# A fused attention and wave layer on one Trainium2 core: first loads, first rotation and slot transfers reordered and joined

## The reference, cut to what matters

```python
x = x + attn(layernorm(x))          # x: 4 x 2048 x 256 f32
x = x + ffn(layernorm(x))
# attn: qkv = x @ w_qkv; 16 heads of 16 dims; rotary embedding on Q and K;
#       softmax(Q K^T / 4, causal) V, then @ w_proj + b_proj
# ffn:  sqrt((x @ cos(theta + theta_noise))^2 + (x @ sin(phi + phi_noise))^2)
```

## Time and profile before

| | |
|---|---|
| median of 3 runs | 2236.44 us (2230.28 to 2236.95) |
| the profiled execution, its own time | 2240.03 us |
| its span, first to last instruction | 2238.3 us |
| mean granted TensorE clock | 0.966 of full speed |
| PE busy | 2070.9 us (93%) |
| VectorE (DVE) busy | 1601.9 us (72%) |
| ScalarE (ACT) busy | 1296.1 us (58%) |
| POOL (GpSimd) busy | 870.6 us (39%) |
| DMA moved | 159.87 MB, 71 GB/s on the mean |

### The profile page before, as it was taken

The page is one execution under the profiler, slowest core; times in us unless marked ns, Lnnn a source line. Parts: engine busy times, 40 slices in busy tenths (PEclk is TensorE's granted clock), DMA queues, the critical chain, the costliest instruction groups (busy, mean ns, idle before and its releaser), DMA issues.

```text
span 2238.3 us, 37555 instructions
## 1 busy us (share of the span) xinstructions
PE 2070.9 (93%) x12864; PEld 869.9 (39%) x12864; DVE 1601.9 (72%) x2868; ACT 1296.1 (58%) x1620; POOL 870.6 (39%) x1250
## 2 busy tenths in 40 slices
PE   4999999989999999999999999999999999999883
PEld 3333333334433344334443344334444344333331
DVE  4787777877778778787677767687777777778611
ACT  1346656655566565666567555665656565566571
POOL 4622324352444325343534434335244434432331
PEclk9889999999999999999999999999999999999996
DMA  5420222132212223222222222122122211221211
GB/s 159 115 62 23 73 61 88 42 103 60 82 55 80 61 61 88 65 84 87 75 70 77 72 65 79 58 75 84 56 77 71 81 60 52 73 72 32 78 58 43
DMA packets 119561, 159.87 MB, mean 71 GB/s; under 512 B 30662, under 2 KB 82246, under 8 KB 119110
## 3 DMA queue, kind: packets, MB, share of 16 engines
q1 hardware_dynamic: 118928, 155.22, 23.7%
q10 hardware_dynamic: 444, 2.26, 0.3%
HBM read 88.97 MB, written 50.86 MB: 62 GB/s over the span
## 4 chain that ended last, share of the span: by engine, by line
PE 62%; DMA 7%; DVE 7%; issue 7%; POOL 7%; ACT 5%; SPq 4%; POOLq 0%; DVEq 0%
PE banks L761 16%; PE banks L745 15%; PE banks L724 15%; PE banks L685 5%; DVE chunk_max L943 4%; PE banks L694 3%; ACT probs L831 3%; DMA rot<-raw 3%; PE banks L675 2%; PE banks L722 2%; DMA inverse<-inverses 2%; SPq L508 2%; PE banks L708 2%; POOL crossed L478 1%; SPq L525 1%
## 5 line engine op out<-in xcount | busy, mean ns | idle before, releaser
L943 DVE TENSOR_REDUCE chunk_max<-banks 128x1 f32<-128x512 f32 (+3 forms) x2240 | 1399.8, 671 | 433.6 <-PE banks L724 418.9
L831 ACT ACTIVATE probs<-banks 128x1024 f32<-128x1024 f32 (+3 forms) x1280 | 1074.7, 899 | 567.5 <-PE banks L745 543.1
L724 PE MATMUL banks<-stack_k,stack_q 96*128 96x512 bf16 (+3 forms) x2560 | 833.7, 357 | 35.3 <-DVE chunk_max L943 27.6
L745 PE MATMUL banks<-stack_q,stack_k 99*128 99x512 bf16 (+3 forms) x2560 | 694.4, 353 | 15.9 <-ACT probs L831 7.0
L761 PE MATMUL banks<-probs,v_one 128*17 128x512 f32 (+3 forms) x5120 | 539.0, 537 | 21.4 <-POOL probs L1078 20.2
L724 PEld LDWEIGHTS banks<-stack_k,stack_q 96*128 96x128 bf16 x2560 | 249.3, 99 | 406.2 <-DVE chunk_max L943 183.5
L745 PEld LDWEIGHTS banks<-stack_q,stack_k 99*128 99x128 bf16 x2560 | 220.9, 99 | 280.7 <-ACT probs L831 127.5
L1078 POOL TENSOR_SCALAR_AFFINE_SELECT probs<-probs 128x512 f32<-128x512 f32 x256 | 166.3, 655 | 314.1 <-ACT probs L831 307.8
L761 PEld LDWEIGHTS banks<-probs,v_one 128*17 128x17 f32 x5120 | 117.7, 97 | 303.0 <-issue 224.2
L722 PE MATMUL banks<-diag_mask,ident_bf 128*128 128x128 bf16 x1024 | 204.9, 225 | 12.7 <-DVE chunk_max L943 9.1
L722 PEld LDWEIGHTS banks<-diag_mask,ident_bf 128*128 128x128 bf16 x1024 | 100.3, 99 | 148.2 <-DVE chunk_max L943 75.3
(11 more groups left out here) (88 smaller groups left out, 1134.3 us busy)
## 6 DMA issues: line engine op xcount, KB each, us to landing
split<-parts SPq DMA_DIRECT2D x64, 384.0 KB, 2.6
stack_q<-split SPq DMA_DIRECT2D x384, 64.0 KB, 2.2
stack_k<-split SPq DMA_DIRECT2D x384, 64.0 KB, 2.2
rot<-raw SPq DMA_DIRECT2D x256, 64.0 KB, 2.0
sums<-o_raw SPq DMA_DIRECT2D x64, 256.0 KB, 2.1
xin<-x SPq DMA_DIRECT2D x16, 512.0 KB, 4.0
heads_t<-sums SPq DMA_DIRECT2D x28, 256.0 KB
mid<-x SPq DMA_DIRECT2D x14, 512.0 KB, 4.1
```

What stands on the lines that cost most here:

```text
L724: mm = nc.tensor.matmul(bank[:, n * wide:(n + 1) * wide], stack_q[u % 2][0:SPLIT_ROWS, t, h + n, j * P:(j + 1) * P], stack_k[u % 2][0:SPLI ...
L745: mm = nc.tensor.matmul(scores_bank[h][:, w0:SPAN], stack_k[u % 2][0:ROWS, j // SUB, h, (j % SUB) * P:(j % SUB + 1) * P], stack_q[u % 2][0 ...
L831: nc.scalar.activation(probs[:, g % PROBS, 2 * pair:2 * pair + 2, w0:SPAN], scores_pair[pair][:, :, w0:SPAN], ACT.Exp).then_inc(s_exp, 1)
L943: nc.vector.tensor_reduce(to, bank[:, 0:count * wide].rearrange("p (h n) -> p h n", h=count), AX.X, ALU.max).then_inc(s_emptied["DVE"], 1)
```

## The change

It does nine things. The statistics of block 1 wait for the normalisation of block 0. The query and key weights are loaded as the first group and the other three, the tables as the first span's columns and the rest; PE and the rotation wait for each at its first use. In the first rotation two of the four half swaps are issued on ScalarE's queue, and its seven VectorE operations are planned with no lag between them. fetch_slots issues six copies where it issued twelve: a run of slots with the same part is one copy with a broadcast source, a run with successive parts one copy with the parts as its first dimension. The value products of a unit wait in the plan for its query and key product, and unit 1's first products for unit 0's rows. The planner's costs of SP's jobs are raised. SLACK goes from 0.2 to 0.4. A change of type on PE is put off within 3 us of the last one (STICK, RUN). The split's result is planned as usable 1.0 us later (TURN_LAG). The change is described as having the value products two steps at a time; VALUES is 2 on both sides of the diff.

```diff
+SLOT_RUNS = ((0, 0, 0, 3, True), (0, 3, 1, 2, True), (0, 5, 2, 1, True), (1, 0, 0, 3, False), (1, 3, 0, 2, False), (1, 5, 0, 1, True))
+HALVES = ((0, 32), (32, 0), (64, 96), (96, 64))
-LOADS = 2 * SLOTS * 16
+LOADS = len(SLOT_RUNS) * 16
-SLACK = 0.2
+SLACK = 0.4
+STICK = 0.05
+RUN = 3.0
+TURN_LAG = 1.0
...
-            job(("xload", n), "SP", 0.1, at, [("xt", n - 2, 1)], 4.2)
-            job(("stats", n), "DVE", 2.1, at, [("xload", n), ("apply", n - 2), begun(at - SLACK)])
+            job(("xload", n), "SP", 0.45, at, [("xt", n - 2, 1)], (4.8, 8.0)[n] if n < 2 else 4.2)
+            job(("stats", n), "DVE", 2.1, at, [("xload", n), ("apply", n - 2), *([("apply", 0)] if n == 1 else []), begun(at - SLACK)])
...
-            job(("rot", u, c), "SP", 0.3, at, [("out", ("qk", u, c, 1)), ("rope", *ago, 1)], 2.4)
+            job(("rot", u, c), "SP", 2.4 if i else 1.2, at, [("out", ("qk", u, c, 1)), ("rope", *ago, 1)], 1.8)
...
-                    job(("rope", u, c, n), "DVE", 0.68, at, after)
+                    job(("rope", u, c, n), "DVE", 0.8, at, after, 0.0 if n < ROPE_OPS - 1 else None)
...
-            job(("keep", u, c), "SP", 0.1, at, [("rope", u, c, ROPE_OPS - 1), ("fetch", *ago)], 2.4)
-            job(("fetch", u, c), "SP", 1.0, at, [("keep", u, c), ("scores", u - 2, NSTEP - 1, 1)], 4.0)
+            job(("keep", u, c), "SP", 0.45, at, [("rope", u, c, ROPE_OPS - 1), ("fetch", *ago)], 2.4)
+            job(("fetch", u, c), "SP", 2.7, at, [("keep", u, c), ("scores", u - 2, NSTEP - 1, 1)], 2.2)
...
-            job(("split", u, c), "POOL", 1.3, at - 0.2, [("rowmax", u, c)])
+            job(("split", u, c), "POOL", 1.3, at - 0.2, [("rowmax", u, c)], TURN_LAG if u else None)
...
-            job(("rows", u, c), "SP", 0.3, at, [("out", ("turn", u, c))], 2.4)
+            job(("rows", u, c), "SP", 1.7, at, [("out", ("turn", u, c))], 1.8)
...
-            found.append((max(at, free[e]) + TURN_COST * change, jobs[name][2], name))
+            stick = STICK * change if free[e] - since < RUN else 0.0
+            found.append((max(at, free[e]) + TURN_COST * change, jobs[name][2] + stick, name))
...
-                    for at in range(0, P, P // 2):
-                        for own, other in ((at, at + 32), (at + 32, at)):
-                            sp.dma_start(rot[own:own + 32, i % 2, :], raw[other:other + 32, i % 2, :]).then_inc(s_rot[i % 2], 16)
+                    for own, other in HALVES[0:2] if i == 0 else HALVES:
+                        sp.dma_start(rot[own:own + 32, i % 2, :], raw[other:other + 32, i % 2, :]).then_inc(s_rot[i % 2], 16)
...
-                    for side, (tile, which) in enumerate(((stack_q, Q_PARTS), (stack_k, K_PARTS))):
-                        for slot, part in enumerate(which):
-                            rows = split[i % 2, part, side * P // 2:(side + 1) * P // 2, :]
-                            sp.dma_start(tile[u % 2][slot * HD:(slot + 1) * HD, c, :, :],
-                                         rows.rearrange("(d h) n -> d h n", h=HG)).then_inc(s_fetch[i % 2], 16)
+                    for side, slot, part, count, same in SLOT_RUNS:
+                        rows = split[i % 2, part:part + (1 if same else count), side * P // 2:(side + 1) * P // 2, :]
+                        if same:
+                            rows = rows.to_broadcast([count, P // 2, SPAN])
+                        tile = (stack_q, stack_k)[side][u % 2][slot * HD:(slot + count) * HD, c, :, :]
+                        sp.dma_start(tile.rearrange("p h n -> p (h n)"), rows.rearrange("m (d h) n -> m d (h n)", h=HG)).then_inc(s_fetch[i % 2], 16)
...
-                sp.dma_start(wqk[:, :, :, :], w_qk.rearrange("g p k n -> p g k n")).then_inc(s_wqk, 16)
+                sp.dma_start(wqk[:, 0, :, :], w_qk[0]).then_inc(s_wqk[0], 16)
                 load_block(1)
                 sp.dma_start(wv[:, :, :], w_v.rearrange("(k p) n -> p k n", p=P)).then_inc(s_wv, 16)
+                sp.dma_start(wqk[:, 1:GROUPS, :, :], w_qk[1:GROUPS].rearrange("g p k n -> p g k n")).then_inc(s_wqk[1], 16)
...
+                        if i == 0:
+                            ins.then_inc(s_emptied["ACT"], 1)
+                            emptied(act, item)
+                            for own, other in HALVES[2:4]:
+                                act.dma_start(rot[own:own + 32, 0, :], raw[other:other + 32, 0, :]).then_inc(s_rot[0], 16)
+                            return
...
-                act.dma_start(cos_t[:, :], cosines).then_inc(s_tables, 16)
-                act.dma_start(sin_t[:, :], sines).then_inc(s_tables, 16)
+                for n, columns in enumerate((slice(0, SPAN), slice(SPAN, SEQ))):
+                    act.dma_start(cos_t[:, columns], cosines[:, columns]).then_inc(s_tables[n], 16)
+                    act.dma_start(sin_t[:, columns], sines[:, columns]).then_inc(s_tables[n], 16)
```

More of the change, by code:

```diff
@@ L166, in plan @@
             for k in range(KT):
-                job(("qk", u, c, k), "PE", 0.86, at - HOLD * k, [("out", ("xt", n, k)), before_qk, ("rope", *ago, 1), begun(at - SLACK)])
+                job(("qk", u, c, k), "PE", 0.86, at - HOLD * k, [("out", ("xt", n, k)), before_qk, ("rope", *ago, 1), begun(at - SLACK), ("rows", u - 1, c) if u == 1 else begun(at - SLACK)])
                 before_qk = ("qk", u, c, k)
             with_bank(("qk", u, c, 0), ("qk", u, c, 1), "ACT", 0.5, at, [("rope", *ago, 1)])
-            job(("rot", u, c), "SP", 0.3, at, [("out", ("qk", u, c, 1)), ("rope", *ago, 1)], 2.4)
+            job(("rot", u, c), "SP", 2.4 if i else 1.2, at, [("out", ("qk", u, c, 1)), ("rope", *ago, 1)], 1.8)
             last = ((i - 1) // SPANS, (i - 1) % SPANS)
@@ L212, in plan @@
             free = [("qk", UNITS - 1, SPANS - 1, KT - 1), ("v", PAIRS - 1, SPANS - 1, SUB - 1)] if finish_set(n) else []
-            job(("den", n), "SP", 0.1, at, [("store", unit, t), ("keepinv", prev), ("den", n - 1), begun(at - SLACK)], 2.2)
-            job(("heads", n), "SP", 0.2, at, [("store", unit, t), ("wave", prev, SUB - 1), ("sin", KT - 1), ("heads", n - 1), *free], 2.5)
-            job(("x3", n), "SP", 0.1, at, [("final", prev), ("x3", n - 1), begun(at - SLACK), *free], 4.2)
+            job(("den", n), "SP", 0.5, at, [("store", unit, t), ("keepinv", prev), ("den", n - 1), begun(at - SLACK)], 2.2)
+            job(("heads", n), "SP", 1.1, at, [("store", unit, t), ("wave", prev, SUB - 1), ("sin", KT - 1), ("heads", n - 1), *free], 2.5)
+            job(("x3", n), "SP", 0.45, at, [("final", prev), ("x3", n - 1), begun(at - SLACK), *free], 4.2)
             job(("bias", n), "POOL", 1.3, at, [("x3", n), ("bias", n - 1)])
             job(("invert", n), "DVE", 0.5, at, [("den", n), ("invert", n - 1)])
-            job(("keepinv", n), "SP", 0.1, at, [("invert", n), ("keepinv", n - 1)], 2.2)
-            job(("inverse", n), "SP", 0.2, at, [("keepinv", n), ("add", prev), ("inverse", n - 1), *free], 2.5)
+            job(("keepinv", n), "SP", 0.35, at, [("invert", n), ("keepinv", n - 1)], 2.2)
+            job(("inverse", n), "SP", 1.1, at, [("keepinv", n), ("add", prev), ("inverse", n - 1), *free], 4.5)
             job(("scale", n), "DVE", 1.25, at, [("heads", n), ("inverse", n), ("scale", n - 1)])
@@ L262, in plan @@
             job(("lift", u, t), "ACT", 0.6, at - 0.1, [before_values])
-            job(("store", u, t), "SP", 0.1, at, [("lift", u, t)], 2.4)
+            job(("store", u, t), "SP", 0.35, at, [("lift", u, t)], 2.4)
     left = {name: len(j[3]) for name, j in jobs.items()}
@@ L274, in plan @@
     held, bank, prior = [None] * RING, {}, {}
-    exact = None
+    exact, since = None, 0.0
     for name, n in left.items():
@@ L301, in plan @@
         if e == "PE":
+            if exact != (name[0] not in COARSE):
+                since = start
             exact = name[0] not in COARSE
@@ L411, in layer_kernel @@
         out_bank = psum[7]
-        s_wqk = sem("query_key_weights_loaded")
+        s_wqk = [sem(f"query_key_weights_loaded{n}") for n in range(2)]
         s_wv = sem("value_weights_loaded")
-        s_tables = sem("rotation_tables_loaded")
+        s_tables = [sem(f"rotation_tables_loaded{n}") for n in range(2)]
         s_corner = sem("diagonal_mask_loaded")
@@ L472, in rope @@
                 emptied(engine, ("qk", u, c, 1))
-                if i == 0:
-                    engine.wait_ge(s_tables, 32)
+                if i < 2:
+                    engine.wait_ge(s_tables[i], 32)
                 ins = ops.tensor_tensor(turned[:, :], raw[:, i % 2, :], cos_t[:, span], ALU.mult)
@@ L693, in project @@
                         bank_of(item)
+                        if u < 2 and c == 0:
+                            pe.wait_ge(s_wqk[u], 16)
                     mm = nc.tensor.matmul(ring[BANK[item]], wqk[:, u % GROUPS, k, :], x_t[:, k, c * SPAN:(c + 1) * SPAN],
@@ L705, in project_values @@
                         bank_of(item)
+                        if q == 0 and c == 0:
+                            pe.wait_ge(s_wv, 16)
```

11 lines of the change are left out of this document (5 added, 6 removed).

## The result

The changed kernel takes 2450.8 us (median of 4 runs, 2442.2 to 2455.2) against 2233.4 for the kernel before beside it: a ratio of 1.0969, interval [1.093, 1.101]. That is 217 us slower where 11 faster were forecast, and far outside the range.

What follows compares the result with a forecast made beforehand. PE was taken to bound the middle, idling at the start. Start -9 and middle -2 (-4 - 6 + 8) took the median from 2236.4 to 2225 us; forecast's own range 2218 to 2233, overall 2207 to 2246.

Steps and rivals of the forecast that it cites:

- Part 1: First block: the normalisation of block 0 can begin at 11.5, 8.1 us gone; waits for weights taken at 0.
- Part 2: First rotation: swap on two queues, operations kept together, no value products between; parts complete at 25.0 us, stored at 27.7.
- Part 3: Joined fetch copies: a leading 3 or 2 uses three or two DMA engines, so a fetch takes 14 us.
- Rival C: Early fetches wait for one another on engine 0, the start's gain shrinks to about 0, middle a draw: 2235; chance 0.24.
- The start, -9: Start of the kernel: time taken out is passed on almost whole, -9 us, ends -6 and -16.
- Part 4 (c): Middle: swaps behind a fetch land later, +8 us (0 to +16); rows, stores and later fetches have some 19 us or more.
- The term for swaps: Middle: 15 of 64 swaps behind a fetch land some 5.5 us later, 83 us of POOL's waiting, taken at +8.
- Rival D: A swap late behind a fetch holds POOL's masks, and PE holds its value products: +14, 2250; chance 0.18.
- Part 4 (d): Middle: longer slack (0.4) and stickiness of PE's type taken at nothing; possible loss named, VectorE dry in fp32 runs.
- (a): Middle: POOL's split gets 1.0 us until the turn may be planned, cutting PE's waits: -4 us (0 to -13).
- (b): Middle: swaps booked with 1.5 us more distance, so 61 us of POOL's waiting could go: -6 us.

Runs made afterwards that it cites:

- e: The changed kernel with twelve fetch copies and the planner's old constants (SLACK, STICK, TURN_LAG, SP's costs), leaving the start alone: 2230.4 us, 1.0003 of the kernel before.
- a: The changed kernel with the twelve fetch copies of before in place of the six joined ones: 2236.3 us, 1.0002 of the kernel before.
- f: The kernel before with the planner's new constants alone (SLACK, STICK, TURN_LAG, SP's costs), twelve fetch copies and the old start: 2242.3 us, 1.0048.
- c: The changed kernel with the three small copies of the rows of maxima issued on ScalarE's queue: 2363.3 us, 1.0577 of the kernel before.
- d: The changed kernel with slots laid out in DRAM by six stores and fetched by two copies of 96 rows: 2226.9 us, 0.9970 of the kernel before.
- l: The changed kernel with twelve fetch copies and STICK at 0: 2188.5 us, 0.9804 of the kernel before.
- o: The wide version with STICK at 0 and TURN_COST at 0: 2171.1 us, 0.9720 of the kernel before.
- p: The changed kernel with twelve fetch copies, STICK at 0 and TURN_COST at 0: 2173.8 us, 0.9731 of the kernel before.
- the wide version: The changed kernel with slots laid out in DRAM by six stores and two fetches of 96 rows; 2226.9 us as first run, further constants varied later.
- i: The changed kernel, joined copies included, with the planner's constants of before: 2271.3 us, 1.0178 of the kernel before.
- b: The kernel before with the six joined fetch copies alone, its planner unchanged: 2286.0 us, 1.0214 of the kernel before.
- m: The changed kernel with its joined copies and STICK at 0: 2370.7 us, 1.0623 of the kernel before.

## Why the prediction was wrong

**Part 1** (first block, -8.1): right. The transposes came 9.7 us sooner, 1.5 of it because POOL's deviation was ready sooner (9.68 against 11.22), which was not in the sum. The value weights did cost a wait, of 1.5 us.

**Part 2** (parts ready at 25.0): 29.1. The operations after the crossed product do follow each other, but a normalisation and block statistics (22.11 to 25.3) still stood ahead of it, and SP issued the second swap first (28.65), both of which I had taken away at full value. The swap's gain on two queues was lost in that.

**Part 3** (a fetch of 14 us): the mechanism was right, and the size nearly, 16.0 for the first, though in part by luck: an engine moved 27 GB/s and not the 20.6 of the earlier trace rows, by which 256 KB take 9.7 us, and the time to the first packet and the bytes of other copies made up the rest. The second span's maximum came at 67.34, not 57. Its own fetch took 14.5 us, as forecast, but was issued at 52.81 and not at 43: the first fetch had begun at 33.87 and not at 27.7, the rotation was done at 41.1 and not at 33, and the store, issued at 42.87, took till then to land. Rival C had this waiting of one copy behind the other.

**The start, -9**: the claim that time taken out of it is passed on almost whole isn't borne out. Run e shows 9.7 us at the first transposes, 3.9 at the end of unit 0, and in the runs nothing that can be told from none; a against f shows 6 to 10 us of it at the end, under the new orders. So what the start is worth depends on the order behind it, and where it goes in e isn't settled.

**Part 4 (c)** is the step that failed, and by far the most: "Rows of maxima, stores and later fetches queue there too, but their users come some 19 us or more later". That lead was worked out from the planner's constants (0.56 unit less 0.43), not from the trace. In the kernel before, the rows of the last span of a unit were issued 3.0 to 17.3 us before their first score, and the third span's came down to 7.0 under the new orders. Run c takes the rows out of the ring, and 87 of the 217 us are gone. The term for swaps was also too small: POOL waits 211.3 us, 113 more than in a, where I had 83. 21 of the 64 swaps begin within 13 us behind a fetch's start, 6.2 us behind it on the mean, where I had 15 and 8.5. What these waits cost PE isn't measured, so the other 130 us are shown to come from the joined copies (a, d), but not by which wait.

**Rival D** named the right place, a copy late behind a fetch and an engine in order, and the sign, but the wrong copy first, and was priced at +14. Its share wasn't a constant, either: PE idles in each wait and then works at the lower clock (0.63 us for the product that took 0.38). Over the kernel its products took 68 us longer, and no term of mine held it.

**Part 4 (d)** was the second failure. "The longer slack (0.4) and the stickiness of PE's type I take at nothing": stickiness is 44 to 48 us (a against l). The possible loss was even named, as VectorE running dry in long fp32 stretches; the starts of PE's products point the other way round, to more maxima in a row when PE is not in fp32, and to the clock; neither was tried by itself. That a change of type costs nothing fits o and p. **(a)**, the lag, taken at -4, measures -6 to -9, hardly clear of noise. **(b)** can't be read alone; but l shows that the new constants without stickiness, together with the start, are worth 2%: the lag some 6 us of it, the longer slack 18 in the wide version, the rest not split. In place of -11 in all, then, stand +214 for the joined copies, +48 for stickiness and -44 for everything else, the start among it.

## What to carry to other kernels

Before copies are joined, look at the slowest dimension of both sides: here a leading 3 or 2 put all bytes on three or two DMA engines, and the small copies issued behind them on the same queue waited. The largest single part of the price was that of the small copies with the least time to spare, so measure the slack of each one in the trace (issue to first use), under the new order, and don't take it from a plan's lead times. In a list scheduler a preference must be paid for by something the trace shows: avoiding changes of type, for which no row showed a cost, lost 2%.

## What the runs showed that was not expected

Three copies of 4 KB, issued 4.3 us behind the start of a fetch, held PE for 9 us, and others of the kind for up to 14.6 us at a time; for the same copies from another queue it waited 2.9 us at most. The same joined copies cost 41 us (i against e), 52 (b), 182 (m against l) and 214 (the change against a) by the order around them. And 2.7% lay in the order of the work alone (p), with every copy as before.
